# A graph attention layer on one core: the order inside TensorE's and ScalarE's step, and a wait on GpSimd's gathers

## The chip, the cores and the metric

The kernel runs on one core of one Trainium2 chip. The time is the device time of one execution, in microseconds; of several executions the median counts.

## The reference

A layer of graph attention over 6250 nodes and 100000 edges, with 128 features, whose edges come sorted by their target `dst`, followed by a residual and a layer norm:

```python
hl = x @ Wl.T + bl
hr = x @ Wr.T + br
s = (hl[src] + hr[dst]) * alpha            # alpha: (100000, 128)
s = where(s >= 0, s, 0.2 * s)
smax = segment_max(s, dst)
e = exp(s - smax[dst])
att = e / segment_sum(e, dst)[dst]
out = layernorm(x + segment_sum(x[src] * att, dst))
```

Everything per edge is element-wise in the 128 features; the softmax runs over the edges of one target node, for each feature by itself.

## The kernel before

**Tiling.** Edges are cut into chunks of 128. A chunk is paired with each block of 128 nodes that its targets touch; four such pairs make a step, and there are 208 steps (`STEPS`). In a step the features of an edge lie in the free dimension, 128 edges on the partitions, four pairs side by side (512 columns).

**Head.** First come the projections of all nodes (left ones are written to DRAM beside x, as rows that can be gathered, right ones stay in SBUF), and tables that say which chunk meets which block. It ends some 50 to 80 us into the span.

**A step k**, by names. GpSimd gathers the rows of the 512 source nodes, four indirect DMAs of 128 rows each (line 389), into one of eight slots of `xg`: half a row is the left projection, half is x. SyncE loads the edges' features `attr` and two kinds of `line`. TensorE makes distances of target numbers into `ps_q` (line 561), from which ScalarE makes the transposed one-hot `onehotT` (line 672); TensorE adds the gathered left rows (line 545) and the right rows picked by `onehotT` (line 549): this is u, in `ps_u`. VectorE multiplies it by `attr` (v, line 933) and applies the leaky slope (s, line 905, both of whose inputs are v in SBUF). TensorE turns s (transposes it) into `ps_sT` (line 538). VectorE runs a scan forward (line 901) and one backward (B, line 912) for the segment maxima, and subtracts (z, line 917). TensorE turns z back into `ps_z` (line 567). ScalarE takes the exp of it into `ex` (line 678) and, in place, into `ps_z` (line 688), with `gap` (line 684) between them; VectorE multiplies the second by the gathered x into the other half of `ex` (line 925, the message product). TensorE makes distances again, the other way round, into `ps_q` (line 589), ScalarE the `onehot` of them (line 701), and TensorE sums exps and messages by node with it (line 580, `ps_w`). ScalarE keeps the sums in `acc` (lines 705, 708), and carries a node that spans two steps on by `had` and `factor` (lines 695, 713, 719).

**Order.** Every engine's order is written out by hand, as a function `body(k)` that holds pieces of several steps. TensorE's body k: turn s of k+1, u of k+3, distances of k+4, turn z of k, sums of k-1, distances of k+1. VectorE's: forward scan of k, s of k+1, B and z of k, message product of k-1, v of k+2. ScalarE's: `onehotT` of k+4, exp, gap, exp of k, then the carried node, `onehot`, `acc`, `factor`, `had`. Engines meet by semaphores: `u_ps` counts finished u, `z_ps` turned z, `msg_ok` message products. GpSimd's loop over the steps has, from step 8 on, one wait, that the message product of step k-8 has freed the slot.

**Tail.** In the last steps ScalarE begins with the reciprocals of the sums, GpSimd multiplies by them right behind its last gather (lines 397, 398), and then come the residual and the layer norm.

Of the kernel before, what the change touches and what calls it, by code (L numbers as in the profile page):

```python
def build_gnn_layer(nc, x, src, dst, edge_attr, w_left, b_left, w_right, b_right, out):
# [6 lines left out]
    ACT = mybir.ActivationFunctionType  # L8
    EngineType = mybir.EngineType

    P = 128
    N, D = x.shape
# [7 lines left out]
    WIDE = 4  # L20
# [11 lines left out]
    LINES = 5  # L32
    EDGES = 8
    FIRST = 6
    FRONT = 16
    BIG = 1.0e38
    SLOPE = 0.2
# [24 lines left out]
    with ctx:  # L62
# [28 lines left out]
        onehotT = sb("onehotT", [P, 2, WIDE * P], bf16)  # L91
# [121 lines left out]
        def has(k):  # L213
            return 0 <= k < STEPS
# [115 lines left out]
        @block.gpsimd  # L330
        def _(pool):
            nc.gpsimd.memset(ident[:, :], 0.0).then_inc(c_id, 1)
            nc.gpsimd.iota(iota_i, [[1, 8], [8, PR]], base=0, channel_multiplier=0).then_inc(c_iota, 1)
            nc.gpsimd.iota(eight_i[:, :], [[1, 8]], base=0, channel_multiplier=8).then_inc(c_iota, 1)
            pool.wait_ge(c_id, 1)
            nc.gpsimd.affine_select(out=ident[:, :], in_=ident[:, :], compare_op=ALU.not_equal, fill=1.0,
                                    base=0, pattern=[[-1, P]], channel_multiplier=1).then_inc(c_id, 1)
            nc.gpsimd.memset(x_all[:, BLOCKS - 1, :], 0.0).then_inc(c_set, 1)
            nc.gpsimd.memset(edge[:, :, :], 1.0).then_inc(edge_set, 1)
            pool.wait_ge(c_id, 2)  # L340
            n_c = [0]

            def after(ins):
                n_c[0] += 1
                ins.then_inc(c_done, 1)
                pool.wait_ge(c_done, n_c[0])

            G = nc.gpsimd

            G.tensor_scalar(minus[:, :], ident[:, :], -1.0, None, ALU.mult).then_inc(c_set, 1)  # L350

            after(G.iota(iota_p[:, :], [[1, P]], base=0, channel_multiplier=0))
            after(G.tensor_copy(iota_n[:, :], iota_p[:, :]))
            after(G.tensor_tensor(n2[:, :], iota_n[:, :], iota_n[:, :], ALU.mult))
            after(G.tensor_copy(node_h[:, :], n2[:, :]))
            after(G.tensor_tensor(n2[:, :], n2[:, :], node_h[:, :], ALU.subtract))
            after(G.tensor_scalar(total[:, :], node_h[:, :], ident[:, 0:1], None, ALU.mult))
            for j, source in ((1, n2), (2, iota_n)):  # L360
                after(G.tensor_scalar(n_part[:, :], source[:, :], ident[:, j:j + 1], None, ALU.mult))
                after(G.tensor_tensor(total[:, :], total[:, :], n_part[:, :], ALU.add))
            after(G.tensor_tensor(node_c[:, :], ident[:, 3:4], ident[:, 4:5], ALU.add))
            G.tensor_scalar(nodeT[:, :], total[:, :], node_c[:, 0:1], None, ALU.add).then_inc(node_ok, 1)
            G.tensor_scalar(node[:, :], total[:, :], node_c[:, 0:1], ident[:, 5:6], ALU.add, ALU.add).then_inc(node_ok, 1)
            pool.wait_ge(c_set, 2)
            G.tensor_copy(minus_b[:, :], minus[:, :]).then_inc(node_ok, 1)

            pool.wait_ge(chunks_out, 96)
            pool.wait_ge(at_ok, 1)  # L370
            for t in range(8):
                pool.indirect_dma_start(  # L372
                    out=pair_i[:, t, :], out_offset=None, in_=chunk_dram,
                    in_offset=bass.IndirectOffsetOnAxis(ap=chunk_at[:, t:t + 1], axis=0),
                ).then_inc(pair_in, 16)

            pool.wait_ge(src_sb, 2)
            for q in range(QUADS):
                pool.wait_ge(rows_out[q], 16)
            for k in range(STEPS):  # L380
                if k == 5:
                    pool.wait_ge(lines_out, 16)
                    pool.wait_ge(more_out, 16)
                    for i in range(FIRST):
                        pool.wait_ge(edge_in[i], 16)
                if k >= SLOTS:
                    pool.wait_ge(msg_ok, k - SLOTS + 1)
                for i in range(WIDE):
                    pool.indirect_dma_start(  # L389
                        out=xg[:, k % SLOTS, i, :], out_offset=None, in_=rows_dram,  # L390
                        in_offset=bass.IndirectOffsetOnAxis(ap=srcT[:, k * WIDE + i:k * WIDE + i + 1], axis=0),
                    ).then_inc(rows_in[k % SLOTS], 16)

            for c in range(CH):
                cols = slice(c * CH * P, (c + 1) * CH * P)
                pool.wait_ge(recip_ok, c + 1)
                G.tensor_tensor(acc[:, 1, cols], acc[:, 1, cols], recip[:, cols], ALU.mult).then_inc(near_ok, 1)
                G.tensor_tensor(acc[:, 0, cols], acc[:, 0, cols], recip[:, cols], ALU.mult).then_inc(near_ok, 1)

        @block.tensor  # L400
        def _(pe):
# [127 lines left out]
            def body(k):  # L529
# [3 lines left out]
                if has(k + 1):  # L533
                    pe.wait_ge(s_ok, k + 2)
                    if k >= 0:
                        pe.wait_ge(z_ok, k + 1)
                    for i in range(WIDE):
                        last = nc.tensor.transpose(ps_sT[:, i * P:(i + 1) * P], s[:, (k + 1) % 2, i, :], ident[:, :])  # L538
                    last.then_inc(sT_ps, 1)
                if has(k + 3):  # L540
                    u, j = ps_u[(k + 3) % 2], (k + 3) % SLOTS
                    if k >= -1:
# [10 lines left out]
                if has(k + 4):  # L553
# [5 lines left out]
                    elif k >= -3:  # L559
                        pe.wait_ge(ohT_ok, k + 4)  # L560
                    nc.tensor.matmul(ps_q[:, :], nodeT[:, :], edge[:, j, :], start=True, stop=True).then_inc(qT_ps, 1)  # L561
                if has(k):
                    pe.wait_ge(z_ok, k + 1)
                    if k >= 1:
                        pe.wait_ge(msg_ok, k)
                    for i in range(WIDE):
                        last = nc.tensor.transpose(ps_z[:, i * D:(i + 1) * D], z[:, k % 2, i * P:(i + 1) * P], ident[:, :])  # L567
                    last.then_inc(z_ps, 1)
                if has(k - 1):
                    if k == STEPS:  # L570
                        opening(1)
# [32 lines left out]
        def _(act):  # L604
# [60 lines left out]
            def body(k):  # L665
                if has(k):
                    places[k] = regs(EngineType.Activation, step_t[96:97, 4 * k:4 * k + 4], LAST)
                if has(k + 4):
                    act.wait_ge(qT_ps, k + 5)
                    if k >= -2:  # L670
                        act.wait_ge(u_ps, k + 3)
                    nc.scalar.activation(onehotT[:, (k + 4) % 2, :], ps_q[:, :], ACT.Relu, bias=ones[:, 0:1], scale=-1.0)\  # L672
                        .then_inc(ohT_ok, 1)
                if has(k):
                    act.wait_ge(z_ps, k + 1)
                    if k >= 2:
# [9 lines left out]

                    act.wait_ge(e_ok, k + 1)
                    nc.scalar.activation(ps_z[:, :], ps_z[:, :], ACT.Exp).then_inc(e2_ok, 1)  # L688
                if has(k - 1):

                    col, new, at, rest = places[k - 1]
# [308 lines left out]
```

## Time and profile before

| | |
|---|---|
| median of 3 runs | 1173.09 us (1171.52 to 1174.13) |
| span of the profiled execution | 1166.5 us |
| TensorE (PE) busy | 1083.9 us, 93% |
| VectorE (DVE) busy | 1081.4 us, 93% |
| ScalarE (ACT) busy | 950.3 us, 81% |
| GpSimd (POOL) busy | 853.4 us, 73% |
| granted TensorE clock, mean | 0.985 |

The span runs from the first to the last instruction that was recorded; the 6.6 us to the median of the runs lie around it. Busy time is what an engine's instructions took. The gap between two instructions of an engine is set down to whatever ended it; "issue" is a gap in which the engine waited for nothing that the profile shows. A gather's time on GpSimd is that of the instruction which writes its descriptors, not of the transfer.

### The profile page before, as it was taken

Reading aid. Unit: us, or ns where it says so; the run is one execution under the profiler, and the core shown is the slowest. Engines: PE = TensorE matmul, PEld = TensorE weight load, DVE = VectorE, ACT = ScalarE, POOL = GpSimd, SP = SyncE. Lnnn points to the kernel's source line nnn. Section 1 sums busy time; section 2 is a strip of 40 time slices with the busy share of each in tenths; the row PEclk is TensorE's granted clock in tenths of the full one; section 3 lists DMA queues with packets and bytes.
Section 4 is the critical chain, followed back from the end, with each engine's and each line's share of the span. In section 5 each row is a group of like instructions: output and inputs, shape, how many; then the busy total and the mean of one; then the engine's idle time right before and its main releaser. Section 6 shows DMA issues by size and latency. Waiting matters only on the chain.

```text
span 1166.5 us, 35708 instructions
## 1 busy us (share of the span) xinstructions
PE 1083.9 (93%) x9359; PEld 903.1 (77%) x9359; DVE 1081.4 (93%) x1466; ACT 950.3 (81%) x2396; POOL 853.4 (73%) x879
## 2 busy tenths in 40 slices
PE   5779999999999999999999999999999999999885
PEld 5648888888788878787887888787877878878763
DVE  6549999999999999999999999999999999999988
ACT  2548888888888888888888888888888888888895
POOL 6477777777777777777777777777777777777772
PEclk9889999999999999999999999999999999999998
DMA  8676666666666666666766666666666666666623
GB/s 221 226 218 194 187 187 189 182 193 189 180 187 185 187 183 187 185 185 186 187 184 181 186 186 184 184 186 178 187 181 183 186 188 184 184 187 185 173 64 110
DMA packets 220971, 213.49 MB, mean 183 GB/s; under 512 B 32765, under 2 KB 193796, under 8 KB 220682
## 3 DMA queue, kind: packets, MB, share of 16 engines
q0 software_dynamic: 40320, 109.96, 33.9%
q1 hardware_dynamic: 180005, 100.86, 31.2%
q8 instruction: 92, 1.51, 0.5%
q14 instruction: 93, 0.76, 0.2%
q10 hardware_dynamic: 461, 0.40, 0.1%
HBM read 200.39 MB, written 11.47 MB: 182 GB/s over the span
## 4 chain that ended last, share of the span: by engine, by line
POOL 55%; issue 19%; PE 15%; DVE 4%; DMA 3%; ACT 2%; SPq 1%; ACTq 0%; DVEq 0%; POOLq 0%
POOL xg L389 54%; PE ps_w L580 5%; PE ps_u L545 3%; PE ps_u L549 2%; PE ps_sT L538 2%; PE ps_z L567 1%; DVE acc L891 1%; DVE stats L962 1%; PE ps_q L561 1%; PE ps_q L589 1%; POOL attr L372 1%; DMA acc<-x_in 1%; DMA attr<-chunk_rows,chunk_at 1%; DMA line<-step_lines 1%; SPq L269 1%
## 5 line engine op out<-in xcount | busy, mean ns | idle before, releaser
L389 POOL DMA_INDIRECT xg<-gather_rows,srcT x832 | 798.8, 960 | 266.8 <-issue 252.1
L580 PE MATMUL ps_w<-onehot,ex 128*128 128x128 f32 x3328 | 407.5, 276 | 3.6 <-ACT acc L708 2.5
L580 PEld LDWEIGHTS ps_w<-onehot,ex 128*128 128x128 f32 x3328 | 389.6, 193 | 4.3 <-issue 4.3
L901 DVE TENSOR_TENSOR_SCAN ps_F<-line,B,ps_sT 128x512 f32<-128x512 bf16 x208 | 266.0, 1279 | 2.0 <-DMA line<-step_lines 1.0
L549 PEld LDWEIGHTS ps_u<-right,onehotT 128*128 128x128 bf16 x2496 | 161.8, 98 | 122.5 <-issue 120.5
L912 DVE TENSOR_TENSOR_SCAN B<-line,ps_F 128x512 f32<-128x512 bf16 x208 | 251.1, 1207 | 0.0
L545 PE MATMUL ps_u<-xg,ident 128*128 128x512 f32 x416 | 219.7, 610 | 26.8 <-DMA xg<-gather_rows,srcT 21.6
L672 ACT ACTIVATE onehotT<-ps_q,ones 128x512 bf16<-128x512 f32 x208 | 142.9, 687 | 67.0 <-PE ps_q L561 46.5
L549 PE MATMUL ps_u<-right,onehotT 128*128 x2496 | 178.2, 220 | 0.0
L925 DVE TENSOR_TENSOR ex<-ps_z,xg 128x512 f32<-128x512 f32 x208 | 142.7, 686 | 32.3 <-ACT ps_z L688 30.3
L705 ACT ACTIVATE acc<-ps_w 128x768 f32 x208 | 170.4, 819 | 0.2
L917 DVE TENSOR_TENSOR z<-ps_sT,B 128x512 f32<-128x512 f32 x208 | 143.8, 691 | 7.2
L933 DVE TENSOR_TENSOR v<-ps_u,attr 128x512 f32<-128x512 f32 x208 | 141.6, 681 | 8.1 <-PE ps_u L549 8.1
L905 DVE SCALAR_TENSOR_TENSOR s<-v 128x512 f32<-128x512 f32 x208 | 144.7, 695 | 0.0
L701 ACT ACTIVATE onehot<-ps_q,ones 128x512 f32<-128x512 f32 x208 | 143.3, 689 | 0.5 <-PE ps_q L589 0.5
L538 PE MATMUL ps_sT<-ident,s 128*128 128x128 f32 x832 | 130.2, 279 | 12.1 <-DVE z L917 8.5
L567 PE MATMUL ps_z<-ident,z 128*128 128x128 f32 x832 | 125.3, 273 | 1.2 <-DVE ex L925 1.2
L688 ACT ACTIVATE ps_z<-ps_z 128x512 f32<-128x512 f32 x208 | 124.1, 597 | 0.0
L678 ACT ACTIVATE ex<-ps_z 128x512 f32<-128x512 f32 x208 | 122.6, 589 | 0.2 <-PE ps_z L567 0.2
L695 ACT ACTIVATE ps_w<-ps_w,had x416 | 80.3, 231 | 46.2 <-PE ps_w L580 42.2
L567 PEld LDWEIGHTS ps_z<-ident,z 128*128 128x128 f32 x832 | 102.1, 141 | 13.7 <-issue 2.7
L538 PEld LDWEIGHTS ps_sT<-ident,s 128*128 128x128 f32 x832 | 87.8, 141 | 30.9 <-issue 21.1
(183 smaller groups left out, 883.7 us busy)
## 6 DMA issues: line engine op xcount, KB each, us to landing
attr<-edge_attr_in SPq DMA_DIRECT2D x832, 64.0 KB
line<-step_lines SPq DMA_DIRECT2D x208, 128.0 KB
xg<-gather_rows,srcT POOLq DMA_INDIRECT x832
gather_rows<-acc SPq DMA_DIRECT2D x12, 512.0 KB, 8.4
edge<-step_lines SPq DMA_DIRECT2D x202, 4.0 KB
acc<-x_in SPq DMA_DIRECT2D x6, 448.0 KB, 6.6
xg<-x_in SPq DMA_DIRECT2D x6, 448.0 KB, 3.8
out<-attr SPq DMA_DIRECT2D x6, 448.0 KB, 3.0
```

The source lines that it names most:

```text
L389: pool.indirect_dma_start(out=xg[:, k % SLOTS, i, :], out_offset=None, in_=rows_dram, in_offset=bass.IndirectOffsetOnAxis(ap=srcT[:, k * W ...
L538: last = nc.tensor.transpose(ps_sT[:, i * P:(i + 1) * P], s[:, (k + 1) % 2, i, :], ident[:, :])
L545: nc.tensor.matmul(u[:, :], ident[:, :], xg[:, j, :, D:ROW], start=True, stop=False)
L549: last = nc.tensor.matmul(u[:, i * D:(i + 1) * D], onehotT[:, (k + 3) % 2, i * P:(i + 1) * P], right[:, bass.ds(at[i], 1), h, :].rearrange ...
L567: last = nc.tensor.transpose(ps_z[:, i * D:(i + 1) * D], z[:, k % 2, i * P:(i + 1) * P], ident[:, :])
L580: last = nc.tensor.matmul(columns, ex[:, (k - 1) % 2, c, i, :], onehot[:, (k - 1) % 3, i, :], start=(i == 0), stop=(i == WIDE - 1), skip_g ...
L701: nc.scalar.activation(onehot[:, (k + 1) % 3, :, :].rearrange("p i n -> p (i n)"), ps_q[:, :], ACT.Relu, bias=ones[:, 0:1], scale=-1.0).th ...
L705: nc.scalar.activation(acc[:, :, bass.ds(rest, (WIDE - 1) * P)], ps_w[:, :, P:WIDE * P], ACT.Copy)\
L901: V.tensor_tensor_scan(ps_F[:, :], line[:, k % LINES, 0:GE], ps_sT[:, :], B[:, (k - 1) % 3, GE - 1:GE], ALU.add, ALU.max).then_inc(F_ok, 1)
L905: V.scalar_tensor_tensor(out=s[:, (k + 1) % 2, :, :].rearrange("p i d -> p (i d)"), in0=v[:, :], scalar=SLOPE, in1=v[:, :], op0=ALU.mult, ...
L912: V.tensor_tensor_scan(B[:, k % 3, ::-1], line[:, k % LINES, GE:0:-1], ps_F[:, ::-1], -BIG, ALU.add, ALU.max).then_inc(B_ok, 1)
L917: V.tensor_tensor(z[:, k % 2, :], ps_sT[:, :], B[:, k % 3, :], ALU.subtract).then_inc(z_ok, 1)
```

## The change

Three edits. GpSimd's gathers of step k wait, from step 5 on, also until u of step k-5 is there (`LEAD = 5`). In TensorE's body the turn of z of k moves from behind the distances of k+4 to ahead of u of k+3. In ScalarE's body `onehotT` of k+4 moves from ahead of the first exp to behind the second. No instruction but the waits is added or taken away.

```diff
--- before.py
+++ after.py
@@ -32,6 +32,7 @@
     LINES = 5
     EDGES = 8
     FIRST = 6
+    LEAD = 5
     FRONT = 16
     BIG = 1.0e38
     SLOPE = 0.2
@@ -383,6 +384,8 @@
                     pool.wait_ge(more_out, 16)
                     for i in range(FIRST):
                         pool.wait_ge(edge_in[i], 16)
+                if k >= LEAD:
+                    pool.wait_ge(u_ps, k - LEAD + 1)
                 if k >= SLOTS:
                     pool.wait_ge(msg_ok, k - SLOTS + 1)
                 for i in range(WIDE):
@@ -537,6 +540,13 @@
                     for i in range(WIDE):
                         last = nc.tensor.transpose(ps_sT[:, i * P:(i + 1) * P], s[:, (k + 1) % 2, i, :], ident[:, :])
                     last.then_inc(sT_ps, 1)
+                if has(k):
+                    pe.wait_ge(z_ok, k + 1)
+                    if k >= 1:
+                        pe.wait_ge(msg_ok, k)
+                    for i in range(WIDE):
+                        last = nc.tensor.transpose(ps_z[:, i * D:(i + 1) * D], z[:, k % 2, i * P:(i + 1) * P], ident[:, :])
+                    last.then_inc(z_ps, 1)
                 if has(k + 3):
                     u, j = ps_u[(k + 3) % 2], (k + 3) % SLOTS
                     if k >= -1:
@@ -559,13 +569,6 @@
                     elif k >= -3:
                         pe.wait_ge(ohT_ok, k + 4)
                     nc.tensor.matmul(ps_q[:, :], nodeT[:, :], edge[:, j, :], start=True, stop=True).then_inc(qT_ps, 1)
-                if has(k):
-                    pe.wait_ge(z_ok, k + 1)
-                    if k >= 1:
-                        pe.wait_ge(msg_ok, k)
-                    for i in range(WIDE):
-                        last = nc.tensor.transpose(ps_z[:, i * D:(i + 1) * D], z[:, k % 2, i * P:(i + 1) * P], ident[:, :])
-                    last.then_inc(z_ps, 1)
                 if has(k - 1):
                     if k == STEPS:
                         opening(1)
@@ -665,27 +668,27 @@
             def body(k):
                 if has(k):
                     places[k] = regs(EngineType.Activation, step_t[96:97, 4 * k:4 * k + 4], LAST)
+                if has(k):
+                    act.wait_ge(z_ps, k + 1)
+                    if k >= 2:
+                        act.wait_ge(sums_ps, k - 1)
+                    nc.scalar.activation(ex[:, k % 2, 0, :, :].rearrange("p i d -> p (i d)"), ps_z[:, :], ACT.Exp)\
+                        .then_inc(e_ok, 1)
+
+                    act.wait_ge(B_ok, k + 1)
+                    if k >= 2:
+                        act.wait_ge(factor_ok, k - 1)
+                    nc.scalar.activation(gap[:, k % 2:k % 2 + 1], B[:, (k - 1) % 3, GE - 1:GE], ACT.Relu,
+                                         bias=B[:, k % 3, 0:1], scale=-1.0).then_inc(gap_ok, 1)
+
+                    act.wait_ge(e_ok, k + 1)
+                    nc.scalar.activation(ps_z[:, :], ps_z[:, :], ACT.Exp).then_inc(e2_ok, 1)
                 if has(k + 4):
                     act.wait_ge(qT_ps, k + 5)
                     if k >= -2:
                         act.wait_ge(u_ps, k + 3)
                     nc.scalar.activation(onehotT[:, (k + 4) % 2, :], ps_q[:, :], ACT.Relu, bias=ones[:, 0:1], scale=-1.0)\
                         .then_inc(ohT_ok, 1)
-                if has(k):
-                    act.wait_ge(z_ps, k + 1)
-                    if k >= 2:
-                        act.wait_ge(sums_ps, k - 1)
-                    nc.scalar.activation(ex[:, k % 2, 0, :, :].rearrange("p i d -> p (i d)"), ps_z[:, :], ACT.Exp)\
-                        .then_inc(e_ok, 1)
-
-                    act.wait_ge(B_ok, k + 1)
-                    if k >= 2:
-                        act.wait_ge(factor_ok, k - 1)
-                    nc.scalar.activation(gap[:, k % 2:k % 2 + 1], B[:, (k - 1) % 3, GE - 1:GE], ACT.Relu,
-                                         bias=B[:, k % 3, 0:1], scale=-1.0).then_inc(gap_ok, 1)
-
-                    act.wait_ge(e_ok, k + 1)
-                    nc.scalar.activation(ps_z[:, :], ps_z[:, :], ACT.Exp).then_inc(e2_ok, 1)
                 if has(k - 1):
 
                     col, new, at, rest = places[k - 1]
```

## Rows read from the trace of the kernel before

**Rows 1.** The page's chain that ended last, share of the span by engine.

```profile
POOL 55%; issue 19%; PE 15%; DVE 4%; DMA 3%; ACT 2%; SPq 1%; ACTq 0%; DVEq 0%; POOLq 0%
```

**Rows 2.** Gathers' line: duration min/median/max, first, last; idle before; who waited.

```profile
L389 POOL DMA_INDIRECT xg<-gather_rows,srcT x832: 942/946/1560, 48.7 to 1099.9; - x167
...
  issue: 252.1, 827
...
  DVE ex L925: 1.2, 4
...
  PE ps_u L545: 21.6, 29
```

**Rows 3.** Timeline: start, duration (us), engine, line, operation; last gather of a step.

```profile
503.82 0.94 POOL L389 DMA_INDIRECT xg<-gather_rows,srcT  x1 [0.30 <-issue]
```

**Rows 4.** Timeline, the same steps, TensorE.

```profile
506.61 0.39 PE L589 MATMUL ps_q<-node,edge 128*128 128x128 bf16 x4
...
507.00 0.63 PE L538 MATMUL ps_sT<-ident,s 128*128 128x128 f32 x4
...
507.46 1.02 PE L545 MATMUL ps_u<-xg,ident 128*128 128x512 f32 x2
...
508.99 0.38 PE L561 MATMUL ps_q<-edge,nodeT 128*128 128x512 bf16 x1
...
509.21 0.60 PE L567 MATMUL ps_z<-ident,z 128*128 128x128 f32 x4
...
509.65 1.95 PE L580 MATMUL ps_w<-onehot,ex 128*128 128x128 f32 x16
...
511.82 0.63 PE L538 MATMUL ps_sT<-ident,s 128*128 128x128 f32 x4
```

**Rows 5.** Timeline, the same steps, VectorE.

```profile
506.16 0.69 DVE L917 TENSOR_TENSOR z<-ps_sT,B 128x512 f32<-128x512 f32 x1
...
506.77 0.68 DVE L925 TENSOR_TENSOR ex<-ps_z,xg 128x512 f32<-128x512 f32 x1
...
507.96 1.28 DVE L901 TENSOR_TENSOR_SCAN ps_F<-line,B,ps_sT 128x512 f32<-128x512 bf16 x1
...
509.15 0.67 DVE L905 SCALAR_TENSOR_TENSOR s<-v 128x512 f32<-128x512 f32 x1
```

**Rows 6.** Timeline near the start: u of step 0, first gather of step 5.

```profile
71.46 1.49 PE L549 MATMUL ps_u<-right,onehotT 128*128 x12
...
74.97 0.94 POOL L389 DMA_INDIRECT xg<-gather_rows,srcT  x1 [0.44 <-issue]
```

**Rows 7.** Timeline: two pairs of s and the gather started after it.

```profile
424.42 0.67 DVE L905 SCALAR_TENSOR_TENSOR s<-v 128x512 f32<-128x512 f32 x1
424.51 1.40 POOL L389 DMA_INDIRECT xg<-gather_rows,srcT  x1 [0.30 <-issue]
...
429.54 0.67 DVE L905 SCALAR_TENSOR_TENSOR s<-v 128x512 f32<-128x512 f32 x1
...
429.96 1.06 POOL L389 DMA_INDIRECT xg<-gather_rows,srcT  x1 [0.30 <-issue]
```

**Rows 8.** Timeline, the steps of rows 3 to 5, ScalarE.

```profile
505.27 0.59 ACT L678 ACTIVATE ex<-ps_z 128x512 f32<-128x512 f32 x1
...
505.93 0.60 ACT L688 ACTIVATE ps_z<-ps_z 128x512 f32<-128x512 f32 x1
...
507.20 0.69 ACT L701 ACTIVATE onehot<-ps_q,ones 128x512 f32<-128x512 f32 x1
...
509.71 0.69 ACT L672 ACTIVATE onehotT<-ps_q,ones 128x512 bf16<-128x512 f32 x1
```

**Rows 9.** Timeline after the last gather.

```profile
1100.86 2.09 POOL L397 TENSOR_TENSOR acc<-acc,right 128x896 f32<-128x896 f32 x1
...
1101.05 1.31 PE L545 MATMUL ps_u<-xg,ident 128*128 128x512 f32 x2 [1.77 <-DMA xg<-gather_rows,srcT]
...
1101.42 4.12 DVE L905 SCALAR_TENSOR_TENSOR s<-v 128x512 f32<-128x512 f32 x1
```

More of the change, by code:

```diff
@@ L667, in body @@
                     places[k] = regs(EngineType.Activation, step_t[96:97, 4 * k:4 * k + 4], LAST)
[L668 to L673, printed above, removed]
                 if has(k):
@@ L688, in body @@
                     nc.scalar.activation(ps_z[:, :], ps_z[:, :], ACT.Exp).then_inc(e2_ok, 1)
+                if has(k + 4):
+                    act.wait_ge(qT_ps, k + 5)
+                    if k >= -2:
+                        act.wait_ge(u_ps, k + 3)
+                    nc.scalar.activation(onehotT[:, (k + 4) % 2, :], ps_q[:, :], ACT.Relu, bias=ones[:, 0:1], scale=-1.0)\
+                        .then_inc(ohT_ok, 1)
                 if has(k - 1):
```

## Prediction

> **What bounds the kernel now.** I read the chain of waits first. It runs through GpSimd's gathers for more than half of the span, and a further fifth is "issue", time in which an engine waited for nothing [rows 1]. The view of the gather's line says why: 832 gathers from 48.7 to 1099.9 us, median 0.946 us each, and nearly all of the idle time before them is "issue", 0.30 us a gather (252.1 over 827). Waits for a free slot (the message product of step m-8) cost 1.2 us in all [rows 2]. So GpSimd issues without a pause, one gather every 0.95 + 0.30 = 1.25 us, a step of four in 5.00 us, and the 1050 us between first and last gather are the kernel's length; about 49 us stand before them and 66 behind. TensorE and VectorE look as full (93% each, in the table), so their own pace is to be had from one undisturbed body of each. TensorE: turn s at 507.00, u 507.46, distances 508.99, turn z 509.21, sums 509.65, next turn s 511.82: 4.82 us [rows 4]. VectorE keeps the same 4.8. Both are 0.18 us a step faster than GpSimd, catch up with it and then wait for data (29 waits of u for a gather, 21.6 us, [rows 2]). Work taken off them shortens nothing between 49 and 1100 us.
>
> **What GpSimd does lose.** 832 x 0.946 is 787.1 us, and the gathers took 832 x 0.960 = 798.7: 11.6 us went to gathers that took longer, 48 of them over 0.96 us. The timeline shows one next to its cause: s on VectorE (line 905) starts at 424.42, a gather 0.09 later, and it takes 1.40 us; another begins 0.42 after an s and takes 1.06 [rows 7]. Both end 1.48 or 1.49 after s began. A gather that starts d after an s, with d under 0.54, ends at s + 1.49, so it costs 0.54 - d; one that started before s costs nothing, and s keeps its 0.67 either way. The other five VectorE operations are not seen in this role. The page "SBUF — State Buffer" of the Trainium skill, section "Who interferes with whom", has the rule: a VectorE instruction with two inputs in SBUF contends with a GpSimd instruction that reads SBUF. s is the only one here with both inputs in SBUF, so the trace agrees; it also says that whoever starts first blocks the other for the whole instruction, which the 0.67 us of an s that begins inside a gather does not bear out.
>
> So the question is where s falls between two gather starts. Take x, the time from the end of a step's last gather to the start of its u. Here the gather ends at 503.82 + 0.94 = 504.76 [rows 3] and u starts at 507.46 [rows 4]: x = 2.70. From u to the next turn of s are 4.36 us (507.46 to 511.82), from a turn of s to the s that VectorE then makes 2.15 (507.00 to 509.15, [rows 4, 5]). s of a step thus starts x + 6.51 after its last gather's end; gathers start 0.30 + 1.25n after it, the ones in question at 9.06 and 10.31. A collision needs s in 8.52 to 9.06 or 9.77 to 10.31, that is x in 2.01 to 2.55 or 3.26 to 3.80. Read so off the timeline for the 154 steps from 50 to 203, x runs from 2.1 to 4.3, its middle half from 2.66 to 3.21: mostly in the gap. 34 of these steps collided, for 7.8 us.
>
> **The change, part by part.**
> *GpSimd's wait.* Gather m now also waits for u of step m-5. The tightest place is the start: step 5 issues at 74.97, and u of step 0 begins its last part at 71.46 and ends at 72.95, 2.0 us earlier [rows 6]. In the steady part, u of m-5 starts x = 2.7 us after the gathers of m-5, four steps (20 us) before gather m; it is done some 15 us early. Behind this wait are queued all later gathers, but it never ends last. Its own issue: a second wait on 203 steps. Step 5 has eight waits more than its neighbours and its gather began 0.44 instead of 0.30 after the one before [rows 6], and step 5 may have waited for the lines' write as well. Bounds: 0 (one wait on steps from 8 on leaves 0.30) to 0.14 x 203 = 28 us. I take 0: the nearest row is the step with one wait.
> *TensorE.* No instruction is added. Turn z (0.44) moves ahead of u. It now needs the message product of step k-1 right after turn s: that product starts 506.77 and takes 0.68 [rows 5], so it ends 507.45, and turn s ends at 507.46; with some 0.1 us for the signal TensorE slips 0.1 behind VectorE once, and then stays there. What it buys: a wait for a gather no longer delays z's turn, the exps and the message product. What it moves: u to next turn of s becomes 4.36 - 0.44 = 3.92.
> *ScalarE.* Both exps ahead of the relu that makes onehotT. Exp to second exp are 0.66 us (505.27 to 505.93), onehot to the first operation of the next body 2.51 (507.20 to 509.71), onehotT takes 0.69 [rows 8]; with 0.5 for the second exp (it takes 0.60, and the next can start a little before its end: an estimate) onehotT ends 2.51 + 0.66 + 0.5 + 0.69 = 4.36 after onehot began. TensorE's distances for onehot must wait for it, since both use ps_q; onehot starts 0.59 after these could (506.61 to 507.20). That makes a ring of 4.36 + 0.59 = 4.95 plus a signal, against 4.82 for TensorE alone; where TensorE waits, the 0.59 shrinks to the 0.39 of the distances. I take 4.9 us a body: under GpSimd's 5.0, so free, but with 0.1 left instead of 0.18. Before, onehotT had 2 us to spare.
> *Phase of s.* u to next turn of s: 3.92 + 0.08 = 4.00. Turn of s to s: 2.15 before; now TensorE is 0.1 to 0.3 behind (not more, as the scan that precedes s by 1.19, 507.96 to 509.15, must follow the 0.63 of the turn: 1.82). I take 1.9. s falls x + 5.9 after the last gather, 0.6 earlier than before; the collision window in x moves to 2.62 to 3.16. The example's 2.70 would cost 0.08. Of the 154 steps, some 75 have x in such a window; at a mean 0.27 that is 20 us against 7.8. But each collision delays the gathers and so lowers x of the next steps, and at the slower drift of 0.1 x stays high longer. Bounds for this stretch: 7.8 (no worse) to 20; I take 13, which adds 5 us. The first 50 steps, where x falls from 13 to 3 and s passes each gather start once, keep their 4 us.
> *The end.* u of step 206 waits 1.77 us for its gather [rows 9], and turn z, sums and the rest stand behind it. With z's turn and exps ahead that stretch gives back 0.5 to 1 us; and s, held 4.12 us there by GpSimd's closing product, starts only 0.56 us after that one: coming earlier it could run free, up to 3.4 us, hidden partly by the late gather. I take 1 us less.
> Sum against the profiled execution: 1166.5 + 5 - 1 = 1170.5. The median of the runs is 6.6 above the span: 1173.1 + 4 = 1177.
>
> **Rivals.**
> (a) *Gap instead of window.* If VectorE is not held back and s is pinned to the turn of s, the spread of x + offset may narrow, or the offset be 0.3 off (5.6: windows 2.9 to 3.5), and the collisions fall. At most the 7.8 go, with 1 to 3 at the end: 1162 to 1171, say 1168. For: waits for data no longer reach VectorE through the exps. Against: half of x lies where I put the window.
> (b) *Locked on the gathers.* Each s lands before a gather start, unabated: 20 us or more instead of 7.8, so 1173 + 12 to 17 = 1185 to 1190. Decides if the offset is 5.9 to 6.2 and x keeps its spread.
> (c) *ScalarE's ring takes over.* If the ring of exps, onehotT, distances and onehot is longer than 5.0 us, its excess counts on every step: at 5.1, 0.1 x 200 = 20 us, 1193. It costs 0.08 to 0.11 short of that now, by two terms that I estimated.
> (d) *The added wait costs an issue slot*: up to 28 us, 1201.
> (e) *Nothing moves*: VectorE keeps its old place relative to the gathers, 1172 to 1175. For: GpSimd alone sets the pace and doesn't change.
>
> **How the numbers follow.** Forecast (1174 to 1182) 0.37; (a) 0.27; (b) 0.12; (c) 0.07; (d) 0.04; (e) 0.13. Differences under 0.2% (2.3 us) can't be told from none. Slower: four fifths of the forecast, (b), (c), (d): 0.53. Same: the rest of the forecast, (e), a little of (a): 0.22. Faster: 0.25. The range leaves out (c) and (d) above and the far end of (a) below: 1165 to 1190. Both signs have weight; the forecast's own range is 1174 to 1182.
>
> **What would show it.** Gathers: still 832, "issue" 0.30 each, no wait for u; busy time over 787 us grows from 11.6 to some 17, and the long gathers begin just after an s. If "issue" grows, (d). If TensorE's distances wait for onehotT in most steps and the last gather ends past 1120 with GpSimd waiting for slots, (c). The message product should hardly wait for the second exp any more, without a gain. If s starts less than 0.54 ahead of a gather in fewer than 30 of the later steps, (a), and my offset is wrong. The prediction fails outright if the gathers' pitch of 1.25 us itself changes.

## The result, and the profile after

The changed kernel takes 1190.18 us (median, 1189.02 to 1191.74) against 1173.24 for the kernel before: a ratio of 1.0157, 95% interval 1.0135 to 1.0178. It is slower by 17 us; I had forecast slower by 4, with a range that ended at 1190.

The profiled execution's span is 1187.7 us, 21.2 more than before. The two executions behind the profiles differ by more than the medians: this one took 1189.77 us, 2.1 above its span, and in the later runs the time is mostly 1.8 to 2.1 us above the span, at most 3.6. So of the 6.6 us between span and median before only some 2 lie around the span; the rest is that the profiled execution of before was one of the quicker ones. The profiles overstate the loss by some 4 us, and show where it lies. Where the 21.2 us are is read from the line of s, one per step, with the time of the first and of the last. After:

```profile
L908 DVE SCALAR_TENSOR_TENSOR s<-v x208: 672/674/1172, 73.1 to 1136.3; 128x512 f32<-128x512 f32 x104
```

and before:

```profile
L905 DVE SCALAR_TENSOR_TENSOR s<-v x208: 671/674/4119, 73.8 to 1115.2; 128x512 f32<-128x512 f32 x104
```

From first to last s are 1063.2 us against 1041.4: 207 bodies of 5.14 us instead of 5.03. Ahead of the first s the changed kernel is 0.7 us earlier, behind the last both need 51.3 or 51.4 us. The whole loss is in the loop, and no part of it in the tail, where I had booked 1 us of gain.

The chain that ended last, by engine, is another one:

```profile
PE 81%; issue 7%; ACT 5%; DVE 3%; DMA 2%; SPq 1%; POOL 1%; ACTq 1%; POOLq 0%
```

TensorE holds 81% of it, where GpSimd held 55% [rows 1]. The share alone proves little: the chain of wait_only below has PE 51% and POOL 9%, and that kernel is as quick as the one before. The view of the gather's line:

```profile
L392 POOL DMA_INDIRECT xg<-gather_rows,srcT x832: 942/947/1450, 49.0 to 1112.8; - x167
...
  issue: 227.9, 748
  DVE ex L928: 21.3, 70
...
  PE ps_u L559: 4.0, 13
```

The gathers are still issued 0.30 us apart; the lines under "issue" are such gaps too, 0.3 us each, which merely fell beside the end of another instruction. But the last gather starts at 1112.8 instead of 1099.9 [rows 2], and nothing waits for a gather any more: u no longer appears as one who waits. So TensorE doesn't wait for GpSimd, and yet GpSimd is 13 us later. It is late by its collisions with s (a gather that starts just after an s takes longer): 832 gathers at a mean 0.975 us are 811.5, 24.4 us over 832 x 0.946, twice the 11.6 of before.

What bounds is seen in two bodies of the changed kernel's timeline. The first distances are those for onehotT, the second ones those for onehot (onehotT is line 690, onehot 704, the sums 583, the second distances 592, turn s 541; line 698 is ScalarE's first operation on the sums):

```profile
500.41 0.67 ACT L690 ACTIVATE onehotT<-ps_q,ones 128x512 bf16<-128x512 f32 x1
...
501.14 0.40 PE L592 MATMUL ps_q<-node,edge 128*128 128x128 bf16 x4
...
501.90 0.63 PE L541 MATMUL ps_sT<-ident,s 128*128 128x128 f32 x4 [0.36 <-issue]
...
504.55 1.95 PE L583 MATMUL ps_w<-onehot,ex 128*128 128x128 f32 x16
...
505.29 0.67 ACT L690 ACTIVATE onehotT<-ps_q,ones 128x512 bf16<-128x512 f32 x1
...
506.33 0.39 PE L592 MATMUL ps_q<-node,edge 128*128 128x128 bf16 x4
506.62 0.39 ACT L698 ACTIVATE ps_w<-ps_w,had  x2 [0.66 <-PE ps_w L583]
506.78 0.63 PE L541 MATMUL ps_sT<-ident,s 128*128 128x128 f32 x4
...
506.92 0.69 ACT L704 ACTIVATE onehot<-ps_q,ones 128x512 f32<-128x512 f32 x1
...
510.64 0.67 ACT L690 ACTIVATE onehotT<-ps_q,ones 128x512 bf16<-128x512 f32 x1
...
511.37 0.40 PE L592 MATMUL ps_q<-node,edge 128*128 128x128 bf16 x4
...
512.13 0.63 PE L541 MATMUL ps_sT<-ident,s 128*128 128x128 f32 x4 [0.36 <-issue]
```

Turn s starts at 501.90, 506.78 and 512.13: a body of 4.88 us and one of 5.35, 5.12 on average. In the long one onehotT starts at 510.64 and ends at 511.31, and the second distances follow at 511.37, late; then turn s starts 0.76 us after them, with TensorE idle for 0.36 ("issue"), where the short body has 0.45.

The ring that makes these waits is closed over two bodies, and it runs through the sums: ScalarE's line 698 waits for them and starts at 506.62; from there ScalarE is busy up to onehotT's end at 511.31, 4.69 us; turn s starts 0.82 later (512.13); from a turn s to the end of the sums behind it are 4.60 (501.90 to 504.55 + 1.95), and 0.12 more to line 698. That is 10.23 us for two bodies, 5.12 for one. In the body between, onehotT ends at 505.96, before TensorE is through with its sums, and holds nothing up.

The total of waits between 400 and 700 us (engine, line, who ended the wait, us, times, longest) has the wait in every second of the 58 bodies:

```profile
ACT ps_w L698 <- PE ps_w L583: 23.8, 55, 0.7
...
PE ps_sT L541 <- issue: 10.5, 29, 0.4
...
PEld ps_q L592 <- ACT onehotT L690: 5.9, 29, 0.5
```

### The profile page after: what moved, and what is told of

It reads as the page before. It is cut to its first block, busy times and chain, and to the rows that moved or that the text cites. A ratio compares the mean times of both kernels' runs of the same rounds, so it can differ in the third digit from the quotient of the medians.

```text
span 1187.7 us, 35908 instructions
## 1 busy us (share of the span) xinstructions
PE 1089.9 (92%) x9359; PEld 902.9 (76%) x9359; DVE 1084.8 (91%) x1466; ACT 956.8 (81%) x2396; POOL 866.2 (73%) x879
## 4 chain that ended last, share of the span: by engine, by line
PE 81%; issue 7%; ACT 5%; DVE 3%; DMA 2%; SPq 1%; POOL 1%; ACTq 1%; POOLq 0%
PE ps_w L583 29%; PE ps_u L555 14%; PE ps_u L559 11%; PE ps_sT L541 10%; PE ps_z L548 7%; PE ps_q L592 5%; PE ps_q L571 4%; ACT acc L708 1%; DVE acc L894 1%; ACT onehotT L690 1%; DVE stats L965 1%; POOL attr L373 1%; DMA attr<-chunk_rows,chunk_at 1%; SPq L270 1%; ACT right L639 1%
## 5 line engine op out<-in xcount | busy, mean ns | idle before, releaser
L392 POOL DMA_INDIRECT xg<-gather_rows,srcT x832 | 811.5, 975 | 267.0 <-issue 227.9
L583 PEld LDWEIGHTS ps_w<-onehot,ex 128*128 128x128 f32 x3328 | 405.5, 192 | 9.8 <-issue 4.5
L559 PEld LDWEIGHTS ps_u<-right,onehotT 128*128 128x128 bf16 x2496 | 158.1, 98 | 120.6 <-issue 120.6
L555 PE MATMUL ps_u<-xg,ident 128*128 128x512 f32 x416 | 215.7, 601 | 1.6 <-issue 1.6
L559 PE MATMUL ps_u<-right,onehotT 128*128 x2496 | 174.5, 220 | 0.0
L690 ACT ACTIVATE onehotT<-ps_q,ones 128x512 bf16<-128x512 f32 x208 | 139.9, 673 | 13.1 <-PE ps_q L571 11.0
L908 DVE SCALAR_TENSOR_TENSOR s<-v 128x512 f32<-128x512 f32 x208 | 140.7, 676 | 0.0
L548 PEld LDWEIGHTS ps_z<-ident,z 128*128 128x128 f32 x832 | 97.8, 142 | 3.0 <-issue 2.8
```

The source lines that it names most:

```text
L392: pool.indirect_dma_start(out=xg[:, k % SLOTS, i, :], out_offset=None, in_=rows_dram, in_offset=bass.IndirectOffsetOnAxis(ap=srcT[:, k * W ...
L555: nc.tensor.matmul(u[:, :], ident[:, :], xg[:, j, :, D:ROW], start=True, stop=False)
L559: last = nc.tensor.matmul(u[:, i * D:(i + 1) * D], onehotT[:, (k + 3) % 2, i * P:(i + 1) * P], right[:, bass.ds(at[i], 1), h, :].rearrange ...
L583: last = nc.tensor.matmul(columns, ex[:, (k - 1) % 2, c, i, :], onehot[:, (k - 1) % 3, i, :], start=(i == 0), stop=(i == WIDE - 1), skip_g ...
```

## The experiments

Three theories. **Ring**: ScalarE's exps, onehotT, TensorE's second distances and onehot follow each other around in more time than TensorE's own 4.82 us; to it belongs that TensorE starts again late after such a wait. **Collisions**: s meets the gathers' starts and GpSimd loses the time. **Wait**: the added wait costs GpSimd something.

### Each edit by itself

`wait_only` is the kernel before with `pool.wait_ge(u_ps, k - LEAD + 1)` alone, `after_no_wait` the changed kernel without it.

> The kernel before with GpSimd's wait for u of step m-5 alone. Theories ring and collisions: the wait is over some 5 us or more before it is asked, 1172 to 1175 us, issue gaps 0.30 us. Theory wait (each added wait costs GpSimd an issue slot, or holds the gathers): 1180 to 1201 us and longer gaps.

> The changed kernel without GpSimd's wait for u of step m-5, both orders changed. Theories ring and collisions: the same as the changed kernel, 1187 to 1193 us. Theory wait: back to 1173.

Measured: wait_only 1171.56 us, ratio 1.0002 (0.9985 to 1.0020); after_no_wait 1190.32, ratio 1.0166 (1.0140 to 1.0192). The wait costs nothing and gives nothing, with either order.

`act_only` has ScalarE's new order alone:

```diff
 def body(k):                                # ScalarE, kernel before
-    ohT(k + 4)
     exp(k); gap(k); exp2(k)
+    ohT(k + 4)
```

> The kernel before with ScalarE's new order alone: both exps ahead of onehotT, TensorE's order as before. Theory ring: the ring stands here too, and the first exp must in addition follow a turn of z that comes 1.3 us later in TensorE's body, so it is at least as long: 5.1 to 5.3 us a body, 1188 to 1225 us, with TensorE's second distances waiting for onehotT in at least half of the steps. Theory collisions: u to the next turn of s is as before, so 1171 to 1178. Theory wait: 1173.

Measured: 1273.60 us, ratio 1.0878 (1.0851 to 1.0905). Its s:

```profile
L905 DVE SCALAR_TENSOR_TENSOR s<-v x208: 673/674/1178, 73.9 to 1221.3; 128x512 f32<-128x512 f32 x104
```

1147.4 us for 207 bodies: 5.54 us each. The time is above the 1188 to 1225 that I expected of the ring and far from the 1171 to 1178 of collisions and 1173 of wait. Of the 54 bodies between 400 and 700 us every one has both the wait for onehotT and TensorE's idle 0.36 us after it:

```profile
PE ps_sT L538 <- issue: 20.0, 55, 0.4
...
PE ps_q L589 <- ACT onehotT L687: 9.3, 54, 0.2
```

The exp must wait for a turn of z that stands behind TensorE's u and distances, onehotT for the exps, the second distances for onehotT, and turn s and the next u stand behind these.

`pe_only` has TensorE's new order alone:

```diff
 def body(k):                                # TensorE, kernel before
     turn_s(k + 1)
+    turn_z(k)
     u(k + 3); distances(k + 4)
-    turn_z(k)
     sums(k - 1); distances2(k + 1)
```

> The kernel before with TensorE's new order alone; ScalarE keeps onehotT ahead of the exps, and GpSimd has no new wait. Theory ring (the loss is ScalarE's: both exps, then onehotT, for which TensorE's second distances wait, and after such a wait TensorE loses another 0.36 us): no such wait here, TensorE's body stays at 4.82 to 4.9 us, GpSimd stays the bound, 1170 to 1182 us. Theory collisions (the loss is GpSimd's: s falls just ahead of the gathers' starts since u to the next turn of s got 0.44 us shorter): this order alone shortens it, so 1185 to 1192 us with GpSimd waiting for nothing. Theory wait: 1173.

Measured: 1191.59 us, ratio 1.0181 (1.0152 to 1.0211), where theory ring as I had put it had 1170 to 1182. The number is that of theory collisions, so the trace has to tell. One body of its timeline (turn z is line 545, first distances 568, onehotT 672, exps 678 and 688, message product 925):

```profile
505.03 0.63 PE L545 MATMUL ps_z<-ident,z 128*128 128x128 f32 x4 [0.28 <-DVE ex L925]
...
506.97 0.10 PEld L568 LDWEIGHTS ps_q<-edge,nodeT 128*128 128x128 bf16 x1
...
507.44 0.69 ACT L672 ACTIVATE onehotT<-ps_q,ones 128x512 bf16<-128x512 f32 x1 [0.57 <-remote]
...
508.03 0.59 ACT L678 ACTIVATE ex<-ps_z 128x512 f32<-128x512 f32 x1
...
508.69 0.59 ACT L688 ACTIVATE ps_z<-ps_z 128x512 f32<-128x512 f32 x1
...
509.32 0.69 DVE L925 TENSOR_TENSOR ex<-ps_z,xg 128x512 f32<-128x512 f32 x1 [0.21 <-ACT ps_z L688]
...
510.15 0.63 PE L545 MATMUL ps_z<-ident,z 128*128 128x128 f32 x4 [0.27 <-DVE ex L925]
```

Every one of the 59 bodies between 400 and 700 us takes 5.12 or 5.13 us (here turn z at 505.03 and 510.15), and TensorE idles 0.28 us ahead of turn z, waiting for the message product, which waited 0.21 for the second exp, which stands behind onehotT, which had waited 0.57 us for the first distances, which stand behind u, which stands behind turn z. (The view says "remote" here, where the record of the distances' matmul is missing; of 59 such waits it names these distances in 30.) That is a ring too, another one: `ps_z` is not free for the next turn before the message product has read it. So TensorE's new order alone costs as much as the whole change; ScalarE's new order opens this ring (in the changed kernel turn z waits for no message product) and closes the other one, and by chance both are 5.12 us long. GpSimd's loss is large here too (812.3 us of gathers), and no run takes it out of this kernel: that it is not the cause is read from these waits and from the changed kernel's test further down, not shown by a run of its own.

### Runs that were held up

Two sets of four runs say nothing about the 17 us: on their chips the kernel before itself took 1824 and 1797 us. ScalarE and what hangs on it stand still for up to 8 us at a time, and the profile gives only "issue" or "remote" as what ended it, as in the kernel of `before_v_psum` (engine, line, who ended the wait, us, times, longest):

```profile
DVE ps_F L901 <- issue: 367.4, 100, 6.7
...
ACT ps_w L695 <- remote: 290.5, 68, 8.1
```

The four kernels took 1644, 1575, 1822 and 1623 us (after_regs_early, after_oht_mid, before_v_psum, after_v_psum) and on the second occasion 1617, 1567, 1795 and 1609. All that bears on the argument is that the long gathers are gone where v lies in PSUM, past the first 60 us. What was expected of the second occasion:

> The kernel of after_regs_early once more: on the chip of its first run all kernels, the one before too (1824 us), were held up by stalls of up to 8 us on ScalarE and TensorE. Expected on a chip where the kernel before takes 1168 to 1176 us. Theory ring with restart: 1172 to 1185 us. Theory bare ring, or collisions: 1187 to 1192.

> The kernel of after_oht_mid once more, for the same reason. Theory ring: 1174 to 1186 us. Theory collisions alone, or a turn of z that waits for the message product: 1185 to 1192.

> The kernel of before_v_psum once more (s from one input in PSUM, leaky slope left out), for the same reason. In its first run no gather of the loop was over 0.96 us, as expected; the time remains to be seen. Theory collisions for the kernel before: 1156 to 1164 us. Rival (the time comes back as waits for late gathers): 1168 to 1174.

> The kernel of after_v_psum once more (the same edit in the changed kernel, leaky slope left out), for the same reason. Theory ring: 1184 to 1191 us. Theory collisions: 1156 to 1168 us.

All four were repeated later, on chips where the kernel before takes 1170 to 1171 us, one of them the chip of the first occasion.

### TensorE's restart

If the idle 0.36 us ahead of turn s is TensorE loading the register values of the next body (eight, from SBUF, at the head of `body(k)`), which is hidden as long as there is work queued and comes to light after a wait, it should go when the load stands elsewhere:

```diff
 def body(k):                                # TensorE, changed kernel
-    numbers = regs(..., step_pe[32:33, k + 3, :], ...)
     turn_s(k + 1); turn_z(k)
     u(k + 3); distances(k + 4)
+    numbers[k + 1] = regs(..., step_pe[32:33, k + 4, :], ...)
     sums(k - 1); distances2(k + 1)
```

> The changed kernel, with TensorE's eight register values of body k+1 loaded ahead of the sums of body k instead of at the start of body k+1; same work, same order of everything else. Theory ring with restart: in the changed kernel every second body is 5.36 us instead of 4.88, of which 0.36 is TensorE doing nothing ahead of turn s after its second distances waited for onehotT; with the loads earlier this gap goes, bodies are 4.9 to 4.97 us, GpSimd is the bound again and its collisions with s count: 1172 to 1185 us. Theory bare ring (the wait for onehotT by itself sets 5.12, whatever the loads): 1187 to 1192. Theory collisions: no change, 1187 to 1192, with TensorE's body unchanged.

> The kernel of after_regs_early once more (the changed kernel, TensorE's register values of the next body loaded ahead of the sums), for a chip on which the kernel before takes 1168 to 1176 us. Theory ring with restart (0.36 us of idle TensorE behind each wait for onehotT, every second body): bodies of 4.9 to 4.97 us, GpSimd the bound again, 1172 to 1185 us. Theory bare ring: 1187 to 1192 us, bodies still 5.12.

Measured (regs_early_3): 1164.74 us against 1170.89, ratio 0.9948 (0.9927 to 0.9969). Below the 1172 to 1185 that theory ring had: this kernel, with the whole change in it and the load moved, beats the kernel before by 0.5%. Two bodies (turn s is line 548, second distances 600, sums 591):

```profile
502.99 0.22 PEld L600 LDWEIGHTS ps_q<-node,edge 128*128 128x128 bf16 x4 [0.19 <-ACT onehotT L698]
502.99 0.40 PE L600 MATMUL ps_q<-node,edge 128*128 128x128 bf16 x4
...
503.22 0.61 PE L548 MATMUL ps_sT<-ident,s 128*128 128x128 f32 x4
...
506.05 1.86 PEld L591 LDWEIGHTS ps_w<-onehot,ex 128*128 128x128 f32 x16 [0.37 <-issue]
...
508.16 0.61 PE L548 MATMUL ps_sT<-ident,s 128*128 128x128 f32 x4
```

```profile
L916 DVE SCALAR_TENSOR_TENSOR s<-v x208: 673/674/1168, 75.1 to 1113.1; 128x512 f32<-128x512 f32 x104
```

Turn s follows the second distances by 0.23 us, no idle time between, after a wait for onehotT as well. TensorE's queue now idles 0.37 us ahead of the sums instead, so bodies are mostly 4.94 to 5.03 us (1038.0 us for 207: 5.01), just GpSimd's pace; u starts 12 to 13 us after its gathers' end all along, s falls clear of the gathers, and they take only 789.6 us. So this run takes away the ring's excess and the collisions together; the two are told apart by after_v_psum_3, below.

That the idle time is the load can be seen directly. The views leave register loads out, but the trace has their records: one `TENSOR_LOAD` a body on TensorE, 0.59 us each. In the changed kernel's long body it starts at 511.37 with the second distances, behind the wait for onehotT, and ends at 511.96; the first weights of turn s follow at 512.10. In the short body it starts at 506.02, among the sums, ends at 506.61, and turn s has lost nothing. In regs_early_3 it runs from 505.32 to 505.91, and the weights of the sums follow at 506.05.

With the load behind the sums, where these cover it, the kernel is `regs_behind_sums`:

> The changed kernel, with TensorE's register values of the next body loaded behind the sums and ahead of the second distances, so that the load runs while TensorE works off the sums and ends before the wait for onehotT does. In regs_early_3 the load ahead of the sums left a gap of 0.2 to 0.4 us there and bodies of 5.00 us. Theory ring with restart: no gap ahead of turn s nor ahead of the sums, bodies 4.88 to 4.95 us while GpSimd is ahead, then GpSimd's 5.0 and collisions with s: 1158 to 1171 us. Rival (the load holds TensorE wherever it stands): bodies 5.0 or more, 1164 to 1190 us.

Measured: 1174.25 us against 1172.62, ratio 1.0018 (1.0001 to 1.0036), 3 us above what I expected. Where TensorE has its data, the bodies are a little under what theory ring said, 4.87 us and without a gap ahead of turn s (402.34 to 407.21). Over all 207 they are 5.06 (s from 73.0 to 1120.0), above the 5.01 of regs_early_3: the quicker TensorE made the slower kernel.

```profile
402.10 0.40 PE L600 MATMUL ps_q<-node,edge 128*128 128x128 bf16 x4 [0.23 <-ACT onehotT L698]
...
402.34 0.61 PE L548 MATMUL ps_sT<-ident,s 128*128 128x128 f32 x4
...
402.54 0.69 ACT L712 ACTIVATE onehot<-ps_q,ones 128x512 f32<-128x512 f32 x1 [0.16 <-PE ps_q L600]
...
403.22 1.02 PE L562 MATMUL ps_u<-xg,ident 128*128 128x512 f32 x2
...
406.24 0.67 ACT L698 ACTIVATE onehotT<-ps_q,ones 128x512 bf16<-128x512 f32 x1
...
406.97 0.40 PE L600 MATMUL ps_q<-node,edge 128*128 128x128 bf16 x4
...
407.21 0.60 PE L548 MATMUL ps_sT<-ident,s 128*128 128x128 f32 x4
...
409.10 0.67 DVE L916 SCALAR_TENSOR_TENSOR s<-v 128x512 f32<-128x512 f32 x1
...
409.22 1.37 POOL L392 DMA_INDIRECT xg<-gather_rows,srcT  x1 [0.30 <-issue]
```

```profile
L392 POOL DMA_INDIRECT xg<-gather_rows,srcT x832 | 804.2, 967 | 267.6 <-issue 215.0 <-DVE ex L936 21.3 <-PE ps_u L566 17.1
```

Here the ring of one body is seen: from onehot (402.54) to onehotT's end (406.91) 4.37 us, 0.06 to the second distances (406.97), and 0.44 from these to onehot (402.10 to 402.54), together 4.87.

TensorE now catches up with the gathers, u waits for them (18.6 us in all), and s (409.10) starts just ahead of a gather, which takes 1.37 us. The gathers' 804.2 us are 17.1 over 832 x 0.946. This is the kernel that my forecast described: the change without the loss that I had overlooked.

### onehotT between the exps

```diff
 def body(k):                                # ScalarE, changed kernel
     exp(k); gap(k)
+    ohT(k + 4)
     exp2(k)
-    ohT(k + 4)
```

> The changed kernel with ScalarE's onehotT between the first and the second exp (behind gap) instead of behind both. Theory ring: onehotT ends 0.5 us earlier in ScalarE's body, the second distances no longer wait for it, and the message product has time to spare for a second exp that is 0.6 us later; TensorE's body 4.82 to 4.9 us, GpSimd the bound, and the collisions of s with the gathers at the new phase count: 1174 to 1186 us. Theory collisions alone: 1187 to 1192, as nothing changes in the place of s. If the turn of z comes to wait for the message product as with TensorE's order alone: 1185 to 1192.

> The kernel of after_oht_mid once more (the changed kernel with onehotT between the first and the second exp), for the same kind of chip. Theory ring: the second distances wait no longer for onehotT, so 1165 to 1186 us, the higher the more s collides with gathers. Theory of a second ring (message product to turn of z, which made 5.13 us a body with TensorE's order alone): the second exp is 0.6 us later, so the message product and the turn of z behind it are late, 1185 to 1200 us.

Measured (oht_mid_3): 1170.08 us against 1170.32, ratio 0.9998 (0.9984 to 1.0013). One activation earlier for onehotT, and the ring of 5.12 us is gone; the other ring did not come back. The time is at the low end of what theory ring had (1165 to 1186; the expectations for the two earlier runs began at 1174); the gathers take 798.8 us, as before. With the register loads behind the sums as well:

> The same register loads behind the sums, with onehotT between the two exps as in oht_mid_3. There TensorE did not wait for onehotT in most bodies, so the loads have nothing to give: 1165 to 1173 us, as oht_mid_3, GpSimd the bound. Rival (the load's place is worth something by itself, waits or not): 1155 to 1163 us.

Measured: 1172.00 us against 1172.62, ratio 0.9995 (0.9982 to 1.0008). In this order, where onehotT comes in time, the loads' place is worth nothing that can be measured.

### The collisions, by themselves

v stays in PSUM, in place of u, and s is made from that one input; the leaky slope is left out, so this measures time alone. TensorE's wait before it writes into a buffer of u moves with it, from v to s.

```diff
-V.tensor_tensor(v, ps_u[(k + 2) % 2], attr, mult)
+V.tensor_tensor(ps_u[(k + 2) % 2], ps_u[(k + 2) % 2], attr, mult)
-V.scalar_tensor_tensor(out=s, in0=v, scalar=SLOPE, in1=v, op0=mult, op1=max)
+V.tensor_scalar(s, ps_u[(k + 1) % 2], 1.0, None, mult)
```

> The kernel before, with v kept in PSUM (in place of u) and s made from it by a multiplication by 1 with one input; the leaky slope is left out, the instruction has the same size. It has no second input in SBUF, so theory collisions for the kernel before (11.6 us of GpSimd's time, all on the path that sets the end): no gather over 0.96 us in the loop, last gather some 11 us earlier, and s in the tail is not held 4 us: 1156 to 1164 us. Rival (long gathers have another cause, or the time comes back as waits for gathers that land late): 1168 to 1174.

> The kernel of before_v_psum once more, for a chip on which the kernel before takes 1168 to 1176 us. Theory collisions for the kernel before: 1156 to 1164 us, no gather over 0.96 us in the loop. Rival (the time comes back as waits for gathers that land late): 1168 to 1174.

> The changed kernel with v in PSUM and s made from it with one input as before_v_psum has it; the leaky slope is left out. Theory ring: TensorE and ScalarE set 5.12 us a body, so 1184 to 1191 us although the 24 us of long gathers vanish; GpSimd runs ahead until it waits for free slots. Theory collisions: the loss goes with them, 1156 to 1168 us.

> The kernel of after_v_psum once more (the changed kernel with s from one input in PSUM, leaky slope left out), for a chip on which the kernel before takes 1168 to 1176 us. Theory ring: the 24 us of long gathers vanish and the time stays, 1184 to 1191 us; GpSimd then runs ahead until slots are lacking. Theory collisions: 1156 to 1168 us.

Measured (before_v_psum_3): 1159.02 us against 1171.29, ratio 0.9891 (0.9851 to 0.9930). Measured (after_v_psum_3): 1188.76 against 1170.32, ratio 1.0164 (1.0147 to 1.0181). The gathers' line of the first and of the second:

```profile
L389 POOL DMA_INDIRECT xg<-gather_rows,srcT x832 | 787.5, 947 | 265.8 <-issue 251.7 <-DMA gather_rows<-acc 12.3 <-DVE ex L924 1.8
```

```profile
L392 POOL DMA_INDIRECT xg<-gather_rows,srcT x832 | 789.2, 949 | 288.4 <-issue 260.4 <-DMA gather_rows<-acc 13.8 <-DVE ex L927 12.9
```

In the kernel before, the 11.6 us of long gathers go (787.5 us of gathers are 832 x 0.947) and the time falls by 12. In the changed kernel 22 us of them go and the time stays: its ratio is that of the changed kernel. Collisions cost the kernel before what I had said, and the changed kernel nothing, since there they lie beside TensorE's ring. This rules out rival (b), too, whose marks the changed kernel bears: over 20 us of long gathers, and a time at the upper end of its 1185 to 1190.

## Why the prediction was wrong

The direction was right, the size was not: +4 forecast, +17 measured. By its steps:

- *What bounds the kernel now*: GpSimd alone, its pace of 1.25 us a gather, and the 11.6 us that s takes from it. Right, and before_v_psum_3 shows the 11.6 by 12 us.
- *GpSimd's wait*: 0, right (wait_only, after_no_wait).
- *TensorE's order*: no work added, right, and the slip of 0.1 us behind the message product "once" holds in the changed kernel. That this order alone would close the ring through `ps_z` (pe_only) I had not seen; it did not bear on the sum, as ScalarE's edit opens it.
- *ScalarE's order*: **this is the step that failed**: "I take 4.9 us a body: under GpSimd's 5.0, so free". The terms that I summed were right: from onehot to onehotT's end 4.38 us in the changed kernel (501.58 to 505.96) where I had 4.36, and the ring of one body is 4.87 in regs_behind_sums. The wait that it makes is small as well, 0.2 us (5.9 us over 29). Missing was a term: what such a wait costs TensorE beyond itself. The register load at the head of its body, hidden as long as matmuls are queued, then sticks out by 0.36 us ahead of turn s. It delays the sums, for which ScalarE waits in its turn, and so the ring that binds is the one over two bodies, 10.23 us, with the load in it once; a body of 4.88 and one of 5.35 alternate. 5.12 in place of 4.9 lies above GpSimd's 5.0, and 0.1 us on 207 bodies is the loss. regs_early_3 moves the load alone, and the whole loss goes.
- The trace of before had the price. In three places there the second distances wait for onehotT. Near the start, at 86.18, turn s behind them has the same 0.36 us, and so it has behind the first reciprocals:

```profile
1097.89 0.40 PE L589 MATMUL ps_q<-node,edge 128*128 128x128 bf16 x4 [0.26 <-ACT onehotT L672]
...
1098.65 0.52 PE L538 MATMUL ps_sT<-ident,s 128*128 128x128 f32 x3 [0.36 <-issue]
```

  Turn s stands 0.76 us behind the distances there, with 0.36 of "issue". I had looked at an undisturbed body only.
- *Phase of s and collisions*: the offset of 5.9 us from u to s was right: in regs_behind_sums u starts at 403.22 and its s at 409.10, 5.88 later. The term was right in size, too, where TensorE is quick enough for it to count: regs_behind_sums loses 17.1 us to long gathers instead of 11.6, the 5 us of my sum, and is 1.6 us slower than the kernel before. In oht_mid_3, at much the same offset, they were 11.7. In the changed kernel itself they are 24.4 us, not the 17 of my sum, and hidden.
- *The end*: 1 us of gain forecast, none found. The s that GpSimd held for 4.12 us is held no more (the longest takes 1.17), but behind the last s stand 51.4 us as before.
- *From span to median*: I took 6.6 us to lie around the span. It is some 2, as said above; the forecast, a difference from the median of before, doesn't depend on it.
- *Rival (c)*, ScalarE's ring, was nearest to the truth, and its price was about right ("at 5.1: 20 us, 1193"). Its signs came only in part: TensorE's distances wait in half of the bodies, not in most, the last gather starts at 1112.8 and not past 1120, and GpSimd waits for no slot, as the collisions slow it instead. I gave (c) 0.07, because I summed the ring's terms and did not ask what happens to an engine that is made to wait. With 0.05 us between 4.95 and 5.0 and two of its terms estimated, a ring that close to the bound deserved more, and the range should have held its 1193.

The kernel regs_early_3, which has the change and the earlier load, is the quickest here that still does all of the layer's work, at 0.9948 of the kernel before.

## What to carry to other kernels

When an order is changed, write down every ring that it closes through a shared buffer, over all engines, and compare its length with the bound; a ring within a few per cent of it is a rival, not a free edit. Follow the ring past one body, too: here the one that bound took two. Add to a new wait what stands unhidden behind it on the waiting engine's own queue, register loads above all, and look in the trace for one place where that wait already occurs. And when one engine issues at a fixed pace, a quicker partner isn't better by itself: it may only be moved into the times at which the two collide.

## What the runs showed of the hardware

- A load of eight register values from SBUF takes TensorE's queue 0.59 us (`TENSOR_LOAD` records, 0.587 to 0.604 in the changed kernel between 300 and 900 us). Next in the program after a wait it left TensorE idle for 0.36 us (0.51 in the weight-load row); with the 16 matmuls of the sums queued it cost nothing, and ahead of the sums it left 0.37 us on the weight queue. The page "DMA: Bandwidth & Descriptors" of the Trainium skill gives, in the section "Latency and other measured facts", a floor of about 600 ns for a `tensor_load`. The trace agrees, with its 0.59 us.
- A gather on GpSimd that starts up to 0.54 us after s, which has both inputs in SBUF, ends 1.48 to 1.50 us after the start of s (110 gathers of the changed kernel), where others take 0.946 us; with its one input from PSUM no gather after the first 60 us took over 0.97 us. Only its start is open to this: of the other gathers none took over 0.97 us, those among them that were running when an s began, and s keeps its 0.67 us.
- Two engines of nearly the same pace can lock onto each other through it. In the changed kernel GpSimd's own pace is 5.00 us a step; the collisions slow it to TensorE's 5.12, and u starts 12.6 to 14.5 us after its gathers' end in steps 50 to 203. With the collisions taken away (after_v_psum_3) that is 14.4 to 16.3 us, and GpSimd's idle time grows by 21 us, from 267.0 to 288.4: some 8.5 of it ahead of a step's first gather, where the wait for a free slot stands, and 12 in nine gaps of 1.4 to 1.7 us inside steps, whose cause stays open.
- On the two chips where the kernel before took 1824 and 1797 us, the variants of the changed kernel were at 0.86 to 0.90 of it, where on others they are at 0.99 to 1.02. What held ScalarE up there is not to be seen in the profile and stays open.
